# A two-layer graph network on one core: last projection by row block, feature norm from a known variance, f16 counts, first expert pair's weights in dead memory, two gather places

## The chip, the cores and the metric

The kernel runs on one core of one Trainium2 chip. The metric is device time in microseconds. The kernel before took 1129.6 us (median of 3 runs, 1129.23 to 1130.72). All matrices are float32 unless said otherwise.

## The reference, cut to what matters

x has 384 rows of 1024 numbers. There are two layers; each adds two branches to x and then a mixture of experts. In layer 0 every row goes to two of eight experts of width 352. Layer 1 is where the change lies:

```python
xn = _layernorm(x)
x = x + _L1_gnn_ref(xn, ...) + _L1_mix_ref(xn[None], ...)[0]
x = x + _L1_ffn_ref(_layernorm(x)[None], ...)[0]

def _L1_mix_ref(inputs, W_Q, W_K, W_V, W_fc, gamma, beta):
    Q, K = sigmoid(inputs @ W_Q), sigmoid(inputs @ W_K)   # 16 heads of 64
    V = inputs @ W_V
    KV = einsum('bnhk,bnhv->bhkv', K, V)
    num, den = einsum(Q, KV), einsum(Q, K.sum(axis=1)) + 1e-08
    out = (num / den) @ W_fc
    x = out + inputs
    return (x - mean(x)) * rsqrt(var(x) + 1e-05) * gamma + beta

def _L1_ffn_ref(x, centroids, w1, b1, w2, b2, gamma, beta):   # 8 experts, 1024 -> 512 -> 1024
    eid = argmax(x @ centroids.T, axis=1)                     # one expert for each row
    xhat = (x - mean(x)) * rsqrt(var(x) + 1e-05)
    h = xhat * gamma[e] + beta[e]                             # e: the row's expert
    y = x + relu(h @ w1[e] + b1[e]) @ w2[e] + b2[e]
    alpha = sigmoid(x @ centroids[e])
    return alpha * y + (1 - alpha) * x
```

The x of `_L1_ffn_ref` is already normalised, so that its second norm is a norm of a norm.

## The kernel before, in words

Every engine has its own program; they are ordered by semaphores alone. The 384 rows are three blocks (b = 0, 1, 2) of 128. Weights come as a stream of 0.5 MB chunks [128 x 1024] into a ring of 8 slots (`ring`, line 369); a slot is loaded again when `chunk_used` tells that PE has read it. All loads of weights stand in order in SP's queue. A chunk holds two products of 128 x 512 for each block of rows; an f32 product is two PE instructions.

**The mix branch of layer 1.** After Q, K and V, DVE builds eight head pairs: `attend(a)` on PE gives numerator and denominator (L1319), DVE divides (L1899 to L1901) and counts `num_taken`. Then comes the projection W_fc, 8 chunks. PE takes the left half of the columns (slots 0 to 3) for all three blocks together (`chunk_N`, L963, banks 2 to 4), then the right half (slots 4 to 7) by block (`block_rows`, L939, banks 5 to 7). DVE adds the residual to the left halves of all blocks, then for each block: right half (L1915), statistics, the reciprocal deviation by a square root on ACT (`seed`, L641) and one Newton step (L1423 to L1430), scale and add into `xr` (L1920, L1921), statistics of `xr`, again the deviation, and `xn` (L1443). After all three blocks DVE takes statistics of `xn` and writes the features to Y[2].

**The routing of layer 1.** As `xn` comes, PE transposes each block (L920), ACT evicts it (L647), PE multiplies by the centroids (`logits`, L928). DVE finds the first maximum (`first_max`, L1647 to L1653) and writes a one-hot matrix A; PE counts the rows ahead of each row with f32 matrices of zeros and ones (`rank_rows`, L1123, L1126); DVE makes one-hot slots (L1703) and PE the lists of rows (`list_rows`, L1134, f16). A list in `idx` (L1681, L1689) lets POOL gather rows of the features from `xs` in DRAM, where ACT's queue stored them (L636). Layer 0 uses the same functions `first_max`, `rank_rows`, `list_rows` and `route`; there `first_max` runs twice.

**The pairs of layer 1.** Experts go two at a time (four pairs, 64 rows for each expert), both at once in the two halves of PE's columns. For a pair: gather into `Xg` (L559), 8 transposes (`turn_pair_rows`, L1390), 16 small activations on ACT with gamma and beta (`pair_rows_T`, L833), up pass (`up_pair`, L1358, 32 instructions, 8 chunks `w1`), 4 transposes (L1170), relu on ACT (L845), down pass (`down_pair`, L1375, 32 instructions, 8 chunks `w2`), the bias rows `b2row` added by DVE (L1735), a store to `ys` (L804). PE's order is: rows of pairs 0 and 1 turned, up 0, rows of 2 turned, hidden 0 turned, up 1, down 0, rows of 3 turned, hidden 1 turned, up 2, down 1, hidden 2 turned, up 3, down 2, hidden 3 turned, down 3. A gather waits until the one place `Xg` has been transposed. At the end POOL gathers back (L559), DVE adds (L1948), and three stores write `out`.

**Weights of the pairs.** `w1` of even pairs goes to the ring, `w2` of even pairs to G; odd pairs use rest of Y, `mask`, `CT`, `xnT` and `rows`. SP loads `w1` of pair 0 as the ring's next group, as the slots come free from W_fc; `w2` of pair 0 after `num_taken` 8, and then, each as its place is dead, `w1` and `w2` of pair 1. `w1` of pair 2 and later is loaded as an up pass frees its place, `w2` as a down pass does; `b2row` has one place, loaded when the pair before has been added (`y_done`), behind the `w2` loads in the queue.

## Time and profile before

| what | us |
|---|---|
| median of 3 runs | 1129.6 |
| the profiled execution's own time | 1129.68 |
| its span, first to last instruction | 1127.9 |
| PE busy | 1004.0 (89%) |
| DVE, ACT, POOL busy | 346.6, 210.2, 319.0 |
| DMA moved | 175.83 MB, mean 156 GB/s |

"Busy" is an instruction's time on its engine; PE's overlaps its weight loads. The chain of waits follows back from the last instruction to what released each step. PEclk is the clock that PE was granted, as a share of 2.4 GHz: 0.50 is 1.2 GHz. The DMA share is the mean over 16 engines.

### The profile page before, as it was taken

What the parts mean: (1) busy time and instruction counts of PE and PEld (TensorE: products, weight loads), DVE (VectorE), ACT (ScalarE), POOL (GpSimd) and SP (SyncE); (2) the same over time, 40 slices, a digit from 0 to 9 for tenths busy, and PEclk for the clock granted to TensorE, in tenths of its full rate; (3) what the DMA queues carried; (4) which work ended last, traced back from release to release, by engine and by line L of the source; (5) the groups of instructions that cost most, each with busy time, mean ns of one, the idle gap of its engine ahead of it and who ended that gap; (6) DMA issues with size and microseconds to landing.
All of it is one profiled execution on the core that took longest, in us unless ns stands there. A gap on an engine that the chain in (4) does not pass through costs nothing.

```text
span 1127.9 us, 9907 instructions
## 1 busy us (share of the span) xinstructions
PE 1004.0 (89%) x3356; PEld 547.4 (49%) x3356; DVE 346.6 (31%) x947; ACT 210.2 (19%) x445; POOL 319.0 (28%) x247
## 2 busy tenths in 40 slices
PE   3999999999999989999779999289999999963983
PEld 2555555555555445444456655144444555452321
DVE  4233472155000458212230111320220555481002
ACT  2113221111111158300111111101011100022410
POOL 3587887788888500000001000200000000001201
PEclk9999999999999999999769999679999999965996
DMA  9956655544544610130638885643232022297994
GB/s 204 254 95 148 130 112 131 146 97 89 135 98 108 214 56 1 38 112 19 242 115 299 327 334 209 218 156 112 94 108 97 7 86 75 74 329 288 380 325 170
DMA packets 64284, 175.83 MB, mean 156 GB/s; under 512 B 22784, under 2 KB 23392, under 8 KB 64112
## 3 DMA queue, kind: packets, MB, share of 16 engines
q1 hardware_dynamic: 39424, 148.13, 40.7%
q0 software_dynamic: 20960, 15.63, 7.9%
q10 hardware_dynamic: 3856, 11.52, 2.7%
q8 instruction: 23, 0.38, 0.1%
q14 instruction: 21, 0.17, 0.0%
HBM read 161.73 MB, written 13.52 MB: 155 GB/s over the span
## 4 chain that ended last, share of the span: by engine, by line
PE 48%; POOL 21%; DMA 11%; issue 9%; DVE 8%; ACT 1%; SPq 0%; DVEq 0%; POOLq 0%
PE bank L963 17%; PE bank L1160 7%; POOL n_hi L506 6%; POOL n_lo L506 6%; PE bank L939 4%; POOL w_lo L506 4%; POOL w_hi L506 4%; PE bank L952 4%; PE bank L1185 3%; PE bank L1375 3%; PE bank L1358 3%; DMA n_hi<-G 3%; DMA n_lo<-count,ridx 2%; DMA Y<-xs,idx 2%; DMA n_hi<-count,ridx 2%
## 5 line engine op out<-in xcount | busy, mean ns | idle before, releaser
L952 PE MATMUL bank<-xnT,ring 128*128 128x384 f32 x896 | 292.0, 486 | 3.6 <-DMA ring<-in_stream 1.7
L952 PEld LDWEIGHTS bank<-xnT,ring 128*128 128x128 f32 x896 | 170.0, 190 | 122.6 <-issue 2.4
L559 POOL DMA_INDIRECT Y<-xs,idx x12 | 11.4, 953 | 576.7 <-DMA xs<-Y 283.5
L963 PE MATMUL bank<-ring,xnT 128*128 128x512 f32 x288 | 126.3, 601 | 0.7 <-ACT xnT L647 0.7
L963 PE MATMUL bank<-ring,Y 128*128 128x512 f32 x240 | 104.7, 594 | 0.8 <-DVE Y L1901 0.8
L963 PEld LDWEIGHTS bank<-ring,xnT 128*128 128x128 f32 x288 | 55.4, 193 | 70.4 <-issue 69.3
L506 POOL DMA_INDIRECT n_lo<-count,ridx x48 | 83.8, 1746 | 18.7 <-issue 13.7
L506 POOL DMA_INDIRECT n_hi<-count,ridx x48 | 80.2, 1671 | 16.2 <-issue 13.7
L952 PE MATMUL bank<-Y,ring 128*128 x256 | 82.7, 486 | 0.0
L1160 PE MATMUL bank<-ring,Y 128*128 128x352 f32 x256 | 79.2, 468 | 0.7 <-issue 0.7
L963 PEld LDWEIGHTS bank<-ring,Y 128*128 128x128 f32 x240 | 45.2, 190 | 58.5 <-issue 56.3
L679 ACT ACTIVATE Y<-bank,sbias,scale 128x384 f32 (+1 forms) x48 | 32.2, 671 | 206.3 <-PE bank L952 206.3
L952 PEld LDWEIGHTS bank<-Y,ring 128*128 128x128 f32 x256 | 48.6, 190 | 33.9
L939 PE MATMUL bank<-ring,Y 128*128 128x512 f32 x144 | 62.7, 593 | 0.0
L1160 PEld LDWEIGHTS bank<-ring,Y 128*128 128x128 f32 x256 | 49.1, 194 | 27.5 <-issue 2.8
L506 POOL DMA_INDIRECT w_lo<-wts,kidx x48 | 52.6, 1096 | 30.4 <-DMA n_hi<-G 16.1
L506 POOL DMA_INDIRECT w_hi<-wts,kidx x48 | 52.6, 1096 | 14.7 <-issue 14.3
L920 PE MATMUL bank<-k,xn 128*128 128x128 f32 x72 | 14.9, 376 | 33.6 <-DVE xn L1443 33.6
L939 PEld LDWEIGHTS bank<-ring,Y 128*128 128x128 f32 x144 | 27.1, 190 | 33.0 <-issue 33.0
L559 POOL DMA_INDIRECT Y<-ys,idx x9 | 8.5, 947 | 112.5 <-DMA ys<-Y 110.4
L1492 DVE SCALAR_TENSOR_TENSOR CT<-rows,keyf,k 128x128 bf16<-128x128 f32 x80 | 22.7, 351 | 47.3 <-DMA rows<-keys 46.4
L1546 DVE SCALAR_TENSOR_TENSOR G<-G,mask 128x1152 f32<-128x1152 f32 x1 | 2.6, 2604 | 102.7 <-DMA G<-n_hi 102.7
(270 smaller groups left out, 1016.0 us busy)
## 6 DMA issues: line engine op xcount, KB each, us to landing
ring<-in_stream SPq DMA_DIRECT2D x144, 512.0 KB, 3.7
ring<-in_up SPq DMA_DIRECT2D x32, 704.0 KB, 5.8
Y<-in_stream SPq DMA_DIRECT2D x18, 512.0 KB, 14.0
G<-in_stream SPq DMA_DIRECT2D x16, 512.0 KB, 12.3
ring<-in_dn SPq DMA_DIRECT2D x7, 1024.0 KB, 5.8
ys<-Y ACTq DMA_DIRECT2D x12, 512.0 KB, 6.9
rows<-keys SPq DMA_DIRECT2D x10, 512.0 KB, 5.6
xnT<-in_stream SPq DMA_DIRECT2D x6, 512.0 KB, 14.9
```

The source lines that it names most:

```text
L506: pool.indirect_dma_start(table, bass.IndirectOffsetOnAxis(ap=at[:, e:e + 1], axis=0), what[:, e:e + 1], None, **how).then_inc(done, 16)
L559: pool.indirect_dma_start(dst, None, src, bass.IndirectOffsetOnAxis(ap=idx[:, col:col + 1], axis=0))\
L679: act.activation(dst, bank[m % 2][:, 0:N], ACT.Identity, bias=bi, scale=sc).then_inc(t_evicted, 1)
L920: last = pe.transpose(bank[i][:, k * P:(k + 1) * P], xn[:, b, (4 * i + k) * P:(4 * i + k + 1) * P], ident)
L939: last = pe.matmul(bank[5 + b][:], lhs(2 * (r % 4) + k, b), ring[:, r, k * 512:(k + 1) * 512], start=(start and r == slots[0] and k == 0), ...
L952: last = pe.matmul(bank[to][:, 0:N], ring[:, r, k * P:(k + 1) * P], rhs(k), start=(k == 0), stop=(k == KB - 1))
L963: last = pe.matmul(bank[2 + 3 * half + b][:], lhs(k0 + k, b), ring[:, r, k * 512:(k + 1) * 512], start=(start and k == 0), stop=(stop and ...
L1160: last = pe.matmul(bank[2 + h][:, 0:F0], x_, W[:, o:o + F0], **se)
L1185: last = pe.matmul(bank[5 + half][:], h_, w_, start=(f == 0), stop=(f == 2))
L1358: last = pe.matmul(bank[2][a * HC:(a + 1) * HC, :], XgT[i % 2][:, 2 * j + k, a * HC:(a + 1) * HC], w1_of[i][4 * a + j][:, k * 512:(k + 1) ...
L1375: last = pe.matmul(bank[5 + half][a * HC:(a + 1) * HC, :], hT[:, 2 * kk + k, a * HC:(a + 1) * HC], w2_of[i][4 * a + j][:, k * 512:(k + 1) ...
L1492: last = stt(junk[:, t, :], src, keyf[:, bass.ds(e, 1)], same, ALU.is_equal, ALU.mult, accum_out=ndup[:, bass.ds(e, 1)])
```

## The change

- The projection W_fc goes by row block: block 0 left half and right half (its first slots need only some of the heads), block 1, block 0's transposes, block 2's left half, block 0's logits, block 2's right half, and then blocks 1 and 2 are transposed and multiplied.
- DVE does each block to the end: after `xn` it takes the variance of `xn` as var x rstd^2 (no statistics pass), and writes that block's features over z in Y[3]. ACT stores each block as it comes. The multiplication by the gamma row stands before the wait for the seed.
- The counts use f16 copies `later16`, `ones16` (257 more columns in `k16`) and a 24-column f16 copy A16 of A; A3 is written after it. `first_max` has one instruction less (the comparison adds 100 itself); `route` reads ranks from the bank at once and one-hot columns start at 1, so that the subtraction goes; copy of ranks and the maximum come after the first slots.
- `w1` and `w2` of pair 0 go to memory that is dead during W_fc (Y[4], `mask`, `CT`, Y[5], G, `rows`) and are loaded between the ring's last chunks; `w1` of odd pairs goes to the ring, `w2` of odd pairs to Y[3], `xnT` and Y[2]; the latter waits for gathers 0 and 1.
- There are two gather places, `Xg` and G[8192:9216]. The rows of pair 1 are turned in the middle of up pass 0. DVE does the second half of the rows' eviction (`v_rows_T`), ACT the first.
- Nine semaphores become three with offsets.

```diff
+        w1_even = thirds(Y[:, 4, :]) + [flat[0][:, 0:1024], flat[1][:, 0:1024], Y[:, 5, 1024:2048], g8[1], g8[2]]
+        w2_even = g8[3:7] + [rows[:, 1, :], g8[0], g8[7], rows[:, 0, :]]
+        w1_odd = [ring[:, r, :] for r in range(SLOTS)]
+        w2_odd = thirds(Y[:, 3, :]) + thirds(flat[2]) + thirds(Y[:, 2, :])[0::2]
+        Xgs = [Xg, g8[8]]
...
-            sp.wait_ge(num_taken, 8)
             for r in range(SLOTS):
+                next_chunk(CH_F1 // 8 - 1, r)
+                if r == 3:
+                    sp.wait_ge(product_taken, PR_NUM + 1)
+                if r >= 3:
+                    for n in range(2 * r - 6, 2 * r - 4):
+                        if n < SLOTS:
+                            load_first_w1(n)
+                        else:
+                            load_w2(0, n - SLOTS)
+            for r in range(2, 5):
+                load_w2(0, r)
+            sp.wait_ge(product_taken, PR_NUM + 8)
+            for r in range(5, 7):
                 load_w2(0, r)
             load_b2(0)
-            for r in range(5):
+            for r in range(SLOTS):
+                sp.wait_ge(chunk_used, CH_F1 - 7 + r)
                 load_w1(1, r)
             sp.wait_ge(xn_ready, 4 * NB)
-            for r in range(6):
-                load_w2(1, r)
-            sp.wait_ge(pe_output, AFF)
-            for r in range(5, 8):
-                load_w1(1, r)
-            sp.wait_ge(xs_stored, 96)
-            for r in range(6, 8):
+            load_w2(0, 7)
+            sp.wait_ge(M1s.gathered, 16)
+            sp.wait_ge(odd_gathered, 16)
+            for r in range(SLOTS):
                 load_w2(1, r)
...
-                    else:
-                        pool.wait_ge(S.xt_ready, 2 * e)
-                    gather(Xg, xs, e, S.gathered)
+                    elif e >= n:
+                        pool.wait_ge(S.xt_ready, 2 * (e - n + 1))
+                    gather(places[e % n], xs, e, S.gathered if e % n == 0 else odd_gathered)
...
+            three_seeds(0)
+            store_features(0)
             evict_block(TP0 + 4 * NB, 0)
+            three_seeds(1)
+            store_features(1)
             evict_block(TP0 + 4 * NB, 1)
+            three_seeds(2)
             evict_block(TP0 + 4 * NB, 2)
+            store_features(2)
...
+            def fc_first_block(half):
+                for r in range(4 * half, 4 * half + 4):
+                    pe.wait_ge(landed[r], arr(4)(r))
+                    if half == 0:
+                        pe.wait_ge(product_taken, PR_NUM + 2 * r + 2)
...
+            for half in range(2):
+                fc_first_block(half)
+            for half in range(2):
+                fc_block(1, half)
+            turn_block(T_FE, 3 * NB, 0)
+            fc_block(2, 0)
+            pe.wait_ge(zf_done, 2)
+            logits(T_FE, cent, NE, 0)
+            fc_block(2, 1)
+            for b in range(1, NB):
                 turn_block(T_FE, 3 * NB, b)
-                if b == 0:
-                    pe.wait_ge(zf_done, NB)
                 logits(T_FE, cent, NE, b)
...
+                    if i == 0 and j == 2:
+                        turn_pair_rows(1)
...
-                v.tensor_reduce(cmax, bank[2][:, 120:128], AX.X, ALU.max)
-                step(v.tensor_copy(rank, bank[2][:, 96:120]))
-                step(stt(posm, rank, 1.0, small(168, 24), ALU.add, ALU.mult))
-                step(ts(posm, posm, -1.0, None, ALU.add))
+                step(stt(posm, bank[2][:, 96:120], 1.0, small(168, 24), ALU.add, ALU.mult))
...
+            def v_rows_T(i):
+                v.wait_ge(M1s.xt_ready, 2 * i + 2)
+                for k in range(4):
+                    for a in range(2):
+                        g = 8 * (2 * i + a) + 4 + k
+                        last = ts(XgT[i % 2][:, 4 + k, a * HC:(a + 1) * HC],
+                                  bank[pair_banks(i)[1]][:, k * P + a * HC:k * P + (a + 1) * HC],
+                                  cols[:, C_GAM + g:C_GAM + g + 1], cols[:, C_BET + g:C_BET + g + 1], ALU.mult, ALU.add)
+                last.then_inc(upper_done, 1)
...
                 aggregate(b)
-                rstd_of(7 + 2 * b, b, b + 1)
+                ts(ve[:, b:b + 1], mv[:, b:b + 1, 1], EPS, None, ALU.add).then_inc(var_ready, 1)
                 step(stt(z3[:, b, :], z3[:, b, :], mv[:, b, 0:1], rows[:, 0, :], ALU.subtract, ALU.mult))
+                rstd_from(7 + 3 * b, b, b + 1)
...
+                step(stt(ve[:, b:b + 1], rstd[:, b:b + 1], rstd[:, b:b + 1], mv[:, b, 1:2], ALU.mult, ALU.mult))
+                ts(ve[:, b:b + 1], ve[:, b:b + 1], EPS, None, ALU.add).then_inc(var_ready, 1)
+                rstd_from(9 + 3 * b, b, b + 1)
+                v.wait_ge(xn_ready, 3 * NB + b + 1)
+                ts(xh[:, b, :], xn[:, b, :], rstd[:, b:b + 1], None, ALU.mult).then_inc(xh_ready, 1)
-            v.wait_ge(xn_ready, 4 * NB)
-            rstds(13, xn)
-            normalise(YN(2), xn, xh_ready)
```

## Rows read from the trace of the kernel before

**Rows 1.** The page, part 1: busy time, share of the span, instructions.

```profile
...
PE 1004.0 (89%) x3356; PEld 547.4 (49%) x3356; DVE 346.6 (31%) x947; ACT 210.2 (19%) x445; POOL 319.0 (28%) x247
...
```

**Rows 2.** The chain of waits, in order of time: start us, us, what.

```profile
...
571.84 4.28 DMA Y<-xs,idx
...
1012.53 10.74 DMA xs<-Y
...
1024.02 7.47 DMA Y<-xs,idx
...
1034.27 4.36 DMA Y<-xs,idx
...
1101.60 8.91 PE bank L1375 x32
...
```

**Rows 3.** Windows: length, busy us (instructions) by engine, PEclk, DMA share, GB/s.

```profile
...
905.00:946.00 41.00, 41.00 (x129) 24.17 (x128) 22.53 (x19) 4.71 (x8) 0.00 (x0) 1.00 0.24 81
...
1017.00:1031.00 14.00, 1.78 (x18) 1.52 (x17) 4.66 (x20) 0.00 (x0) 0.96 (x1) 0.50 1.03 415
...
1044.00:1051.00 7.00, 7.00 (x40) 2.98 (x38) 0.69 (x1) 0.90 (x5) 0.00 (x0) 1.00 0.87 307
1051.00:1079.00 28.00, 28.00 (x138) 10.04 (x136) 2.67 (x4) 12.71 (x48) 7.95 (x4) 1.00 1.03 413
...
1096.00:1101.00 5.00, 0.00 (x0) 0.00 (x0) 0.79 (x2) 1.52 (x8) 0.00 (x0) 0.75 0.27 74
...
```

**Rows 4.** Timeline of DVE at the end of pair 2.

```profile
...
1100.21 1.29 DVE L1735 TENSOR_TENSOR Y<-bank,Y 128x512 f32<-128x512 f32 x2 [11.65 <-DMA Y<-in_b]
...
```

**Rows 5.** Timeline of PE: start us, us, engine, line, operation, tiles, count.

```profile
...
524.35 1.04 PE L920 MATMUL bank<-k,xn 128*128 128x128 f32 x8
...
532.09 1.86 PE L928 MATMUL bank<-wqkv,xnT 128*128 128x24 f32 x16
...
565.72 2.73 PE L1123 MATMUL bank<-Y,k 128*128 128x8 f32 x12 [6.89 <-DVE Y L1824]
568.30 1.43 PE L1126 MATMUL bank<-Y,k 128*128 128x8 f32 x6
...
949.26 19.15 PE L963 MATMUL bank<-ring,Y 128*128 128x512 f32 x44 [0.82 <-DVE Y L1901]
...
1006.70 3.58 PE L928 MATMUL bank<-cent,xnT 128*128 128x8 f32 x16 [0.69 <-ACT xnT L647]
...
1021.27 0.40 PE L1134 MATMUL bank<-k,Y 128*128 128x1 f16 x9 [1.52 <-DVE Y L1703]
...
1040.57 8.69 PE L1358 MATMUL bank<-ring,Y 128*64 128x512 f32 x32
...
1066.00 7.09 PE L1358 MATMUL bank<-ring,Y 128*64 128x512 f32 x32
...
```

**Rows 6.** Timeline of DVE around the routings and the last projection.

```profile
...
571.40 0.16 DVE L1681 CAST idx<-bank 128x1 uint32<-128x1 f32 x1 [0.34 <-PE bank L1134]
...
952.30 0.56 DVE L1901 TENSOR_TENSOR Y<-bank,Y 128x384 f32<-128x384 f32 x1
...
975.32 0.69 DVE L1915 TENSOR_TENSOR Y<-bank,xn 128x512 f32<-128x512 f32 x1 [3.19 <-PE bank L939]
...
983.88 0.81 DVE L1443 TENSOR_SCALAR xn<-xr,mv,rstd 128x1024 f32<-128x1024 f32 x1
...
1003.18 0.81 DVE L1443 TENSOR_SCALAR xn<-xr,mv,rstd 128x1024 f32<-128x1024 f32 x1
...
1012.41 0.17 DVE L1933 COPY Y<-bank 128x24 f32<-128x24 f32 x1
...
```

**Rows 7.** DMA issues, 515 to 556 us: KB each, median us to landing.

```profile
...
xs<-xn ACTq DMA_DIRECT2D x3, 512.0 KB, 2.7
...
```

**Rows 8.** Timeline of ACT: the eviction of pair 1's transposed rows.

```profile
...
1039.83 4.83 ACT L833 ACTIVATE Y<-bank,cols 128x64 f32<-128x64 f32 x16 [2.31 <-PE bank L1390]
...
```

**Rows 9.** Timeline of SP: the first reload of weights in the pairs.

```profile
...
1044.16 6.05 SPq L451 DMA_DIRECT2D ring<-in_stream  x8
...
```

More of the change, by code:

```diff
@@ L86 @@
 T_FE = T_Q + 8
+D_FC = NB - 1
+N_K = 2 * NB
+N_V = N_K + 2 * NB
+PR_KV = 2 * NB
+PR_NUM = PR_KV + 8
 EW, GL, G2, ZE, EL, AF = range(1, 7)
@@ L931, in logits, with block_rows @@
                     last.then_inc(pe_output, 1)
-            def block_rows(b, slots, lhs, arrived, start, stop):
+            def block_rows(b, slots, lhs, arrived, start, stop, half=1):
                 for r in slots:
@@ L938, in block_rows @@
                     for k in range(2):
-                        last = pe.matmul(bank[5 + b][:], lhs(2 * (r % 4) + k, b), ring[:, r, k * 512:(k + 1) * 512],
+                        last = pe.matmul(bank[2 + 3 * half + b][:], lhs(2 * (r % 4) + k, b), ring[:, r, k * 512:(k + 1) * 512],
                                          start=(start and r == slots[0] and k == 0),
@@ L1293, in _ @@
             for half in range(2):
-                pe.wait_ge(v_done, 3 * half + 3)
+                pe.wait_ge(hkv_done, N_V + 3 * half + 3)
                 for b in range(NB):
@@ L1328, in _, with attended, fc_block @@
             attend(7)
-            def fc_first(k, b):
-                if k == 0 and b == 2:
-                    pe.wait_ge(num_taken, 7)
-            for kk in range(4):
-                if kk == 3:
-                    pe.wait_ge(num_taken, 8)
-                chunk_N(kk, tok(2), 2 * kk, 0, arr(4)(kk), kk == 0, kk == 3, fc_first if kk == 0 else None)
-            for b in range(NB):
-                block_rows(b, range(4, 8), tok(2), arr(4)(4), True, True)
-            for b in range(NB):
+            def attended(k):
+                return tok(2)(k, 0)
+            def fc_first_block(half):
[3 more added lines that the diff above has]
+                        pe.wait_ge(product_taken, PR_NUM + 2 * r + 2)
+                    for k in range(2):
+                        last = pe.matmul(bank[2 + 3 * half][:], attended(2 * (r % 4) + k), ring[:, r, k * 512:(k + 1) * 512],
+                                         start=(r % 4 == 0 and k == 0), stop=(r % 4 == 3 and k == 1))
+                last.then_inc(block_done, 1)
+            def fc_block(b, half):
+                block_rows(b, range(4 * half, 4 * half + 4), tok(2), 0, True, True, half)
+            for half in range(2):
[8 more added lines that the diff above has]
+            for b in range(1, NB):
                 turn_block(T_FE, 3 * NB, b)
-                if b == 0:
-                    pe.wait_ge(zf_done, NB)
                 logits(T_FE, cent, NE, b)
@@ L1665, in one_hot_slots @@
                 for b in range(NB):
-                    last = ts(slot[:, b, e, :], iota[:, 0:CAP], where[:, b * 8 + e:b * 8 + e + 1], None, ALU.is_equal)
+                    last = ts(slot[:, b, e, :], iota[:, 1:CAP + 1], where[:, b * 8 + e:b * 8 + e + 1], None, ALU.is_equal)
                 return last
@@ L1746, in b2_arrived @@
                     v.wait_ge(b2_in, 32 * i + 32)
+                for i in range(2):
+                    v_rows_T(i)
                 v_hidden(M1s, 0, 1, step)
+                v_rows_T(2)
                 for i in range(1, PAIRS):
@@ L1822, in _ @@
             first_max(lg3, m2, oh2)
-            tt(A3, oh1, oh2, ALU.add).then_inc(R0.assigned, 1)
+            tt(A16, oh1, oh2, ALU.add).then_inc(R0.assigned, 1)
+            step(tt(A3, oh1, oh2, ALU.add))
             tt(dlt, m2, m1, ALU.subtract).then_inc(act_input, 1)
```

195 lines of the change are left out of this document (98 added, 97 removed).

## The prediction

> **What bounds the kernel now.** I read part 1 of the page, then the chain of waits over the last 180 us, then the stretches by window, and last the instructions of PE and DVE one by one there. The page shows PE busy for 89% of the span [rows 1], so most of the kernel is matmul time which the change leaves alone. The chain shows where it is not: from the last projection to the end it leaves PE for DVE, for the store of the features (10.74 us), for two gathers (7.47 and 4.36 us), and then for the last down pass at 1101.60 [rows 2]. The windows say why the store and the first gather are long: the DMA engines are full (415 GB/s, share 1.03) from 1017 to 1031, PE's granted clock is 0.50 there, while from 905 to 946 the same engines had stood at 0.24 [rows 3]. From 1051 on they are full again at 413 GB/s, and the end of that backlog, the bias rows of pair 2, is what DVE waits for at 1100.21, and down pass 3 for DVE [rows 3, 4]. So the tail has two limits in turn: latency up to the first pair, DMA bytes after it.
>
> **The change part by part.** All times are in the old trace's us until the sum.
>
> Layer 0's routing. Nine f32 rank products (18 instructions) run from 565.72 to 569.73, 4.01 us, nothing beside them [rows 5]. In f16 they are 9 instructions. The nearest row is the f16 list product, nine instructions of one column in 0.40 us; the far bound is that an f16 instruction costs what an f32 one does, 9 x 0.22 = 2.0 us. I take 0.5 by the nearer row: gain 3.5. Each first_max loses one instruction at 0.21 (two calls: 0.42); in `route` the copy of the ranks and the subtraction leave the path (0.3 + 0.2 = 0.5), the copy and the maximum now lie under PE's list product. Added: one A3 sum, under the rank products. Sum 4.4 (2.9 to 4.6). The expert loop behind it keeps PE busy without waits for DMA, so I let this stay gained; its cover is PE's alone.
>
> Constants. 257 more f16 columns are 66 KB, 0.16 us at the full rate of [rows 3], at a lower one early on perhaps 0.5; behind them wait the table fills that release POOL. I take 0.3 lost (0 to 0.6). Merging semaphores costs nothing: the same increments in the same order.
>
> The projection. 96 instructions at 0.435 us [rows 5] remain 41.8 us. It starts at 946.6: slots 0 to 2 of block 0 take 5.2 us to 951.8, slot 3 waits for DVE's last head at 952.86 [rows 6], stall 1.1 where the old order had 0.8. Block 0 is whole at 961.5 (it was at 975.3), block 1 at 975.3; then block 0's transposes (0.87 at the full clock), half of block 2, block 0's logits (1.7) [rows 5] and the other half: 991.8 instead of 989.0. PE's path is 2.8 longer, but only DVE needs it. DVE takes 9.37 from the second half's addition to xn (975.32 to 984.69) [rows 6]; now the product with the gamma row covers the seed, about 0.4 less: 8.95. Block 0 has xn at 970.5, its features 2.5 later (two small ops 0.4, seed and Newton steps 1.3, the 0.8 multiplication); block 1's features are ready at 986.8; block 2's first half is taken by 988.2 and DVE then waits for PE until 991.8. Its xn comes at 1000.8 (old 1003.99) and its features at 1003.3 (old 1012.50, after three statistics passes and a common multiplication, just as DVE turned to the logits at 1012.41 [rows 6]). ACT is in order too: block 1's eviction must be over before the seed of block 2; by PE's times it is, by 0.2 us, at 993.7. If it is late, DVE waits that much.
>
> The store. Blocks 0 and 1 are stored earlier; the last starts at 1003.6. The DMA engines then hold nearly nothing (next step), so I take the 2.7 us of layer 0's stores [rows 7] and some issue time, 3 in all, instead of 10.74 [rows 2]: 1006.6. This is no longer last: the list of rows is.
>
> Routing of layer 1. Transpose, eviction and logits of block 2 took from 1003.99 to 1010.3 [rows 5, 6]; now from 1000.8 to 1007.1. DVE is free and copies at once; assignment to rank took 1.67, less 0.2: 1008.6. Rank 0.5: 1009.15 (bound 1010.65). From the end of the rank products to the written index layer 0 shows 1.83 [rows 5, 6]; less 0.5: 1010.45. The gather lands 4.55 after the index in layer 0 (571.56 to 576.12) [rows 2, 6]: 1015.0 against 1031.5. The second list is known 1.9 after the first and the second gather has a place of its own, so it doesn't wait for transposes: landed 1016.9 against 1038.63.
> Beside this the Trainium skill (SBUF — State Buffer, section SBUF: two separate sides) says that a DVE operation in a two-port mode locks GpSimd out, and with it the writing of a gather's descriptors. Layer 0's row disagrees here: that gather landed in 4.28 us with f16 one-hot operations all through it [rows 2]. By the rule the first gather could lose the 1.35 us of the second one-hot operation; by the row nothing. I add nothing.
>
> First pair. Transposes 1.97 at the low clock: 1017.0. The eviction is split: ACT's 8 at 0.30 [rows 8], DVE's 8 of 128x64 out of PSUM are not in the trace; between 0.15 (smallest operations) and 0.45 (128x512 takes 0.69) each, I take 0.2: 1.6. Up pass 0 starts at 1018.6 (old 1040.57). It took 8.69, the first part at clock 0.5, full by 1044 [rows 3, 5]; with pair 1's transposes inside (1.0) and a slightly longer slow part, its end is 1028.6 against 1049.27: PE is 20.7 ahead. Gather 2, which PE needs there, now starts at 1017.3 into full queues: by the first gather's 7.47 us [rows 2] at 1024.8, and even behind the whole 4.2 MB at 1028.9, 0.3 late. From there each pass is 7.0 as before [rows 5].
>
> Weights. Pair 0 (16 chunks of 0.5 MB, save one) is loaded from about 917 to 960, at three chunks per 6.45 us, 244 GB/s in place of 81, under the 413 that the engines reach [rows 3]; ring chunks come first in each round, and need a slot freed by PE, as before: no cost. Pair 1's first weights go into the ring between 978 and 996. Pair 1's second weights wait for both gathers: from 1016.9. Here is the price. Before, all of pair 1 was in place when pass 0 began; now 4.2 MB are still to come and gather 2 is 0.5 MB more: 4.7 MB / 0.413 = 11.4 us of extra backlog. The old backlog ran from the first reload at 1044.16 [rows 9] to the bias rows at 1100.21 [rows 4], 56.0 us, of which 1044 to 1051 moved 307 instead of 413 GB/s, a loss of 1.8 that won't recur as the queue is never empty. New end: 1016.9 + 56.0 - 1.8 + 11.4 = 1082.5. PE's feeding on the way: pair 1's second weights land by 1028.6 (needed 1052), pair 2's first by 1040 (1045.9), pair 3's first by 1050 (1060), pair 2's second by 1061.5 (1067): all in time. PE alone would reach down pass 3 at 1076.4 (its last hidden rows were evicted at 1097.5, the old waits for pair 2 were 0.5); the bias rows let DVE finish pair 2 at 1083.8, so **the last down pass starts 17.7 us earlier** than 1101.60, again after a pause and at the low clock, so it again takes 8.91 [rows 2]. All after it is unchanged, 26.3 us to the span's end.
>
> Sum: 17.7 + 4.4 - 0.3 = 21.8. Span 1127.9 - 21.8 = 1106.1; the profiled run's own time is 1129.68, 1.78 above its span and 0.08 above the median of 1129.6: **1107.9 us**.
>
> **Rivals.**
> A. PE sets the end. The bias rows are 0.5 MB at the tail of a queue; if they pass the weights, or the queue empties sooner, down pass 3 starts at 1076.4 plus nothing: 25.2 instead of 17.7, time 1100.4. For: PE is that far ahead. Against: DVE sat idle 11.65 us for such rows [rows 4], with a smaller backlog beside the same PE work.
> B. Latency ahead of the gathers. Everything behind gather 1 shifts one for one. If the order on ACT and DVE (a seed behind an eviction behind PE's transposes) delays block 2, if f16 rank costs 2.0 in both layers, or if the store still meets loads, 4 to 7 us return: 1112 to 1115, middle 1113.
> C. Nothing comes of it: pair 1's loads, started late, give back all. The backlog would have to last 22 us longer, 9 MB at 413 GB/s; I find 4.7. Time 1129 or so.
> D. Slower: PE's clock. PE idles more thinly spread before pass 0 now; if the granted clock stays at 0.5 (1.2 GHz) through the pairs, each of the seven passes before the last down pass takes 14 instead of 7: it starts at about 1076.4 + 45 = 1121, and itself takes 14 instead of 8.9: end 1127.9 + 20 + 5 - 4 = 1149, time about 1150. It decides from the third slow pass on. Against: at the same point, with the same kind of work, the clock was back by 1044 and stayed at 1.00 to 1079 [rows 3].
> The Trainium skill (TensorE: Matmul & The Clock Gate, section Seeing it yourself) notes a clock seen stuck at a low level for a long time; no row here shows that.
>
> **How the numbers follow.** Forecast 0.62, A 0.16, B 0.14, C 0.03, D 0.05. The likeliest case's own bounds: rank and routing 1.7, eviction 1, backlog 2: 1104 to 1112. With A and B the range is 1099.5 to 1114. A difference over 0.2% is about what can be told from none here (2.3 us): faster 0.92, same 0.03, slower 0.05.
>
> **What the profile after would show.** Rank products of about 0.5 us in both layers; the feature store 3 us; both gathers before the first up pass, 2 us apart; DMA at 0.5 or more from 917 to 946 (old clock) and nearly none from 1000 to 1012; up pass 0 starting 26 us earlier by its own trace; DMA full from then to about 1078, and DVE waiting for bias rows once more before down pass 3. Wrong would be: a PE wait inside the projection, a wait of PE on weights of pairs 1 to 3, DVE waiting for ACT's seed of block 2, or no wait before down pass 3 (A).

## The result and the profile after

The changed kernel takes 1112.14 us (median of 4 runs, 1111.22 to 1114.94) against 1130.16 for the kernel before on the same chip (4 runs, 1129.23 to 1133.93): ratio 0.9834, interval 0.9813 to 0.9855. The forecast was 1107.9, with a range of 1099.5 to 1114. The profiled execution took 1111.84, its span is 1110.0 (before: 1129.68 and 1127.9), so the span lost 17.9 us where the forecast's sum says 21.8.

The measured time is at the upper edge of the forecast's own bounds (1104 to 1112) and also in the band of rival B (1112 to 1115), so the time alone doesn't decide between them; the traces have to.

Two numbers organise all that follows. **Upstream**: DVE's last head ends at 952.86 before [rows 6] and 949.73 now: 3.1 us gained. **Tail**: from there to the end of the span, 175.0 us before, 160.3 now: 14.8 gained. In the experiments the tail is counted from PE's next product, 0.12 us later; there the changed kernel has 160.15. Times of the new trace plus 3.1 are in the clock of the prediction.

The page, part 1, after (as [rows 1]): PE's work is only 5.5 us less, of a gain of 17.9. Most of the gain is waiting.

```profile
PE 998.5 (90%) x3338; PEld 539.8 (49%) x3338; DVE 351.5 (32%) x979; ACT 201.4 (18%) x415; POOL 319.7 (29%) x247
```

The chain of waits after, in order of time (start us, us, what), over the same stretch as [rows 2]:

```profile
949.85 8.82 PE bank L1365 x20
958.67 13.73 PE bank L966 x32
...
1007.75 5.58 DMA Y<-xs,idx
1013.37 1.13 PE bank L1396 x4
1014.53 2.48 ACT Y L855 x8
...
1017.59 5.13 PE bank L1416 x16
...
1058.61 7.02 PE bank L1416 x32
1065.62 4.43 issue
1070.05 9.63 PE bank L1433 x32
...
1080.31 1.75 ACT Y L867 x8
1082.06 2.10 issue
1084.16 8.80 PE bank L1433 x32
```

The store of the features, 10.74 us in [rows 2], is gone from the chain; of the gathers only the first is left in it, 5.58 us instead of 7.47. Up pass 0 starts at 1017.59 (1020.7 in the old clock, 1040.57 before [rows 5]). Then PE runs without a gap to 1065.62, and then the chain shows "issue" of 4.43 and 2.10 us ahead of down passes 2 and 3. A bank that DVE has not emptied yet shows as issue here; DVE's timeline (start us, us, engine, line, operation, tiles, count, idle before and releaser) says why it had not:

```profile
1068.66 1.29 DVE L1782 TENSOR_TENSOR Y<-bank,Y 128x512 f32<-128x512 f32 x2 [16.77 <-DMA Y<-in_b]
...
1082.77 1.29 DVE L1782 TENSOR_TENSOR Y<-bank,Y 128x512 f32<-128x512 f32 x2 [12.22 <-DMA Y<-in_b]
```

The kernel before had both waits too, pair 2's in [rows 4] and pair 1's here, but pair 1's rows came late by so little that down pass 2 lost only 0.51 us (1087.56 to 1088.07):

```profile
1086.67 1.29 DVE L1735 TENSOR_TENSOR Y<-bank,Y 128x512 f32<-128x512 f32 x2 [12.85 <-DMA Y<-in_b]
```

Now PE is ready for down pass 2 22 us sooner and the bias rows of pair 1 come only 18 us sooner, and the same wait costs down pass 2 4.43 us. The windows (length, busy us and instructions of PE, PEld, DVE, ACT, POOL, then PEclk, DMA share, GB/s) show the transfers' side, to be held against [rows 3]:

```profile
917.00:946.00 29.00, 29.00 (x90) 16.70 (x89) 17.81 (x16) 3.24 (x5) 0.00 (x0) 1.00 0.71 257
1003.00:1009.00 6.00, 1.97 (x25) 1.71 (x25) 3.68 (x14) 0.22 (x1) 1.25 (x1) 0.50 0.00 0
1015.00:1029.00 14.00, 11.75 (x56) 5.00 (x56) 5.51 (x20) 4.64 (x16) 4.44 (x4) 0.80 0.94 362
1029.00:1061.00 32.00, 32.00 (x156) 11.45 (x154) 6.19 (x18) 9.79 (x40) 4.44 (x2) 1.00 1.03 410
1061.00:1067.00 6.00, 4.62 (x22) 1.29 (x18) 0.00 (x0) 0.00 (x0) 0.00 (x0) 1.00 1.05 226
1077.00:1083.00 6.00, 3.27 (x18) 1.11 (x14) 0.23 (x1) 1.74 (x8) 0.00 (x0) 1.00 0.44 102
1068.00:1074.00 6.00, 3.95 (x10) 1.37 (x12) 1.89 (x3) 0.00 (x0) 0.00 (x0) 0.53 1.03 410
```

Read the last two columns together. From 917 the loads of pair 0 run under the projection at 257 GB/s, and PE is busy for all 29 us. From 1003 to 1009 nothing moves: the first gather finds the engines empty. From 1017 on they are full. But from 1061 to 1067 the share is 1.05 and the rate only 226 GB/s: full engines that carry half. This is where the two loads of the bias rows of pair 1, 64 partitions each, stand in the queue; they are 0.5 MB of the 1.4 MB that move in these 6 us. The kernel before has the same dip ahead of the same rows:

```profile
1079.00:1086.00 7.00, 7.00 (x36) 2.41 (x34) 0.00 (x0) 1.74 (x8) 0.00 (x0) 1.00 1.03 260
```

Last, PE and POOL around the two routings (same columns as DVE's timeline):

```profile
565.66 0.32 PE L1149 MATMUL bank<-Y,k 128*128 128x8 f16 x6 [6.48 <-DVE Y L1887]
565.84 0.22 PE L1152 MATMUL bank<-Y,k 128*128 128x8 f16 x3
...
571.83 1.97 PE L1171 MATMUL bank<-k,Y 128*128 128x128 f32 x8 [0.69 <-DMA Y<-xs,idx]
574.53 10.78 PE L1186 MATMUL bank<-ring,Y 128*128 128x352 f32 x26 [0.73 <-issue]
```

```profile
1007.40 1.35 DVE L1750 TENSOR_TENSOR Y<-k,Y 128x1152 f16<-128x1152 f16 x1
```

```profile
1007.75 1.83 POOL L580 DMA_INDIRECT Y<-xs,idx  x1 [270.75 <-DVE idx L1728]
1009.89 0.94 POOL L580 DMA_INDIRECT G<-xs,idx  x1 [0.31 <-issue]
```

The rank products take 0.4 us instead of 4.01 [rows 5]. And POOL's first gather instruction takes 1.83 us, the second 0.94; the first one started inside DVE's long one-hot operation.

### The profile page after: what moved, and what is told of

Read it like the earlier page. It is cut to its first block, busy times and chain, and to the rows that moved or that the text cites. A ratio compares the mean times of both kernels' runs of the same rounds, so it can differ in the third digit from the quotient of the medians.

```text
span 1110.0 us, 9830 instructions
## 1 busy us (share of the span) xinstructions
PE 998.5 (90%) x3338; PEld 539.8 (49%) x3338; DVE 351.5 (32%) x979; ACT 201.4 (18%) x415; POOL 319.7 (29%) x247
## 4 chain that ended last, share of the span: by engine, by line
PE 51%; POOL 23%; issue 9%; DVE 8%; DMA 7%; ACT 2%; ACTq 0%; DVEq 0%; POOLq 0%
PE bank L990 15%; PE bank L1186 7%; POOL n_hi L527 7%; POOL n_lo L527 7%; PE bank L966 6%; POOL w_lo L527 4%; POOL w_hi L527 4%; PE bank L979 4%; PE bank L1211 3%; PE bank L1433 3%; PE bank L1416 3%; DMA n_hi<-count,ridx 3%; PE bank L1078 2%; PE bank L1323 1%; DMA Y<-xs,idx 1%
## 5 line engine op out<-in xcount | busy, mean ns | idle before, releaser
L527 POOL DMA_INDIRECT n_lo<-count,ridx x48 | 82.7, 1722 | 17.7 <-issue 13.7
L990 PE MATMUL bank<-ring,Y 128*128 128x512 f32 x192 | 83.6, 594 | 0.0
L966 PE MATMUL bank<-ring,Y 128*128 128x512 f32 x160 | 70.0, 593 | 0.0
L1186 PEld LDWEIGHTS bank<-ring,Y 128*128 128x128 f32 x256 | 49.5, 196 | 27.8 <-issue 3.4
L990 PEld LDWEIGHTS bank<-ring,Y 128*128 128x128 f32 x192 | 36.2, 190 | 46.0 <-issue 45.8
L966 PEld LDWEIGHTS bank<-ring,Y 128*128 128x128 f32 x160 | 30.0, 190 | 35.9 <-issue 35.9
```

The source lines that it names most:

```text
L527: pool.indirect_dma_start(table, bass.IndirectOffsetOnAxis(ap=at[:, e:e + 1], axis=0), what[:, e:e + 1], None, **how).then_inc(done, 16)
L966: last = pe.matmul(bank[2 + 3 * half + b][:], lhs(2 * (r % 4) + k, b), ring[:, r, k * 512:(k + 1) * 512], start=(start and r == slots[0] a ...
L990: last = pe.matmul(bank[2 + 3 * half + b][:], lhs(k0 + k, b), ring[:, r, k * 512:(k + 1) * 512], start=(start and k == 0), stop=(stop and ...
L1186: last = pe.matmul(bank[2 + h][:, 0:F0], x_, W[:, o:o + F0], **se)
```

## The experiments

The theories. **Theory 1**: the end is set by the bytes queued behind gather 1, and by the bias rows at their tail; the shortfall against the forecast lies in the slow bias loads, either because their source is one row broadcast to 64 partitions (1a) or because a load of 64 partitions carries half (1b). **The rival**: it is latency ahead of the gathers (evictions, the collision on POOL) that came back late, and everything behind shifts with it. All ratios are against the kernel before, run on the same chip; the kernel as changed has 0.9834. As upstream varies by some us from profile to profile, the tails of the profiles (160.15 as changed) are a second comparison. A tail is one execution, and it holds the last down pass, which took from 7.11 to 9.94 us in the variants of the changed kernel as the granted clock in it differed; so the table behind the experiments also gives the start of down pass 3.

**All of the first pair's eviction on ACT.** DVE's half (`v_rows_T`) goes back to ACT.

```diff
-            def v_rows_T(i):
-                v.wait_ge(M1s.xt_ready, 2 * i + 2)
...
+                for h in range(2):
+                    act.wait_ge(M1s.xt_ready, 2 * i + h + 1)
+                    for k in range(4):
+                        for a in range(2):
+                            last = act.activation(...)
```

> The changed kernel with one part undone: ACT evicts all 16 pieces of a pair's transposed rows, DVE none. Theory 1 (the end is set by the bytes queued behind gather 1; PE runs ahead and waits): up pass 0 starts about 2.4 us later than 1017.6 (8 more activations at 0.3), but the last down pass starts within 0.5 us of 1084.2 and the time stays within 0.7 us of 1112. Rival (PE's chain from the first pair on sets the end): the time grows by the same 2.4 us, and the last down pass starts at 1086.6.

Measured: 1111.78 us (4 runs, 1108.79 to 1113.73), ratio 0.9832 (0.9802 to 0.9862), tail 161.1. The chain of that kernel:

```profile
1017.74 2.46 issue
1020.20 5.72 PE bank L1417 x16
...
1068.83 2.65 issue
1071.47 8.78 PE bank L1434 x32
...
1082.64 2.72 issue
1085.36 8.80 PE bank L1434 x32
```

Up pass 0 waits longer and starts 1.8 us later than with the split by that profile's own upstream (2.6 less 0.8), and down pass 2 then waits 2.65 instead of 4.43. The delay was eaten by slack before the bytes' end: the rival falls for delays behind the gathers, theory 1 stands.

**Bias rows repeated in DRAM.** Same two loads of 64 partitions, but each of their rows read from its own copy.

```diff
-                    sp.dma_start(b2row[a * HC:(a + 1) * HC, :], b2_d[2 * i + a].to_broadcast([HC, D]))
+                    sp.dma_start(b2row[a * HC:(a + 1) * HC, :], b2_d[2 * i + a, 0:HC, :])
```

> The changed kernel, but each expert's bias row lies 128 times in DRAM (laid out beforehand), so that the load reads 64 different rows instead of one row 64 times; same bytes, same place in the queue. In the changed kernel the DMA rate falls from 412 to about 225 GB/s for 6 us from 1061 to 1067, when the bias rows of pair 1 move. Theory 1a (reading one DRAM row 64 times is slow, 2.7 us for each pair beyond its bytes): the dip goes, the bias rows of pair 1 land about 3 us earlier (1065.5), down pass 2 starts within 1.5 us of up pass 3's end (it had waited 4.4), the rows of pair 2 about 5 us earlier; total 4 to 6 us less. Rival (the low rate comes from the destination, 64 partitions, or from a store beside it): nothing changes, within 0.7 us.

Measured: 1110.19 us (4 runs, 1109.44 to 1113.25), ratio 0.9836 (0.9807 to 0.9864), tail 160.9: nothing. Its window 1059 to 1065 (columns as above):

```profile
1059.00:1065.00 6.00, 4.80 (x24) 1.35 (x20) 0.00 (x0) 0.00 (x0) 0.00 (x0) 1.00 1.03 222
```

Theory 1a falls: the dip is there without a broadcast.

**Bias rows of a pair in one load.** Laid out beforehand as 128 rows for each pair, one load of 128 partitions; the bytes are the same.

```diff
-                for a in range(2):
-                    sp.dma_start(b2row[a * HC:(a + 1) * HC, :], b2_d[2 * i + a].to_broadcast([HC, D]))
+                sp.dma_start(b2row, b2p_d[i]).then_inc(b2_in, 16)
```

> The changed kernel, but the bias rows of a pair come in one load of 128 partitions from a DRAM tensor laid out beforehand, in place of two loads of 64 partitions; same bytes, same place in the queue. With repeated rows but two loads of 64 partitions the dip of the DMA rate had stayed (186 to 260 GB/s for 6 us). Theory 1b (a load into 64 partitions moves at half rate or less; the Trainium skill, SBUF — State Buffer, section Door 1: The DMA port swizzle, says that a range of 64 partitions reaches half of the ports): no dip, rows of pair 1 land 2 to 3 us earlier, rows of pair 2 about 5; last down pass at 1079 to 1080 instead of 1084.2, total 4 to 5 us less than the changed kernel's 1112. Rival (the rate falls because of what else is in flight, stores and descriptors): within 0.7 us.

Measured: 1107.6 us (4 runs, 1105.87 to 1109.25), ratio 0.9777 (0.9733 to 0.9821), tail 156.7. A window, then the chain:

```profile
1059.00:1065.00 6.00, 6.00 (x30) 1.87 (x26) 0.00 (x0) 0.97 (x5) 0.00 (x0) 1.00 1.03 410
```

```profile
1065.21 1.31 issue
1066.52 7.09 PE bank L1431 x32
...
1075.98 3.18 issue
1079.17 9.94 PE bank L1431 x32
```

At the same share of 1.03 the engines carry 410 instead of 222 GB/s, the wait for pair 1's rows shrinks to 1.31 us, and down pass 2 takes 7.09 instead of 9.63, all of it at the full clock. Down pass 3 starts 4.65 us sooner, counted as the tail is; its own clock fell, it took 9.94 instead of 8.80, and so the tail shows 3.45 of that. Theory 1b stands, with two reservations: the edit changes the width of a load and the number of loads together, and by time alone the intervals of the ratios just overlap (0.9821 and 0.9813). That these loads are slow doesn't yet make them the reason why the forecast missed; the point on the backlog below says why they are not. This is also what the Trainium skill says (SBUF — State Buffer, section Door 1: The DMA port swizzle): a transfer to 64 partitions reaches only half of the ports. The trace agrees (226 against 410 GB/s), and adds that such loads in a full queue about halve the rate of the whole core, not only their own.

**Pair 1's second weights loaded as their places die**, partly ahead of the gathers, instead of all after gather 1.

```diff
-            sp.wait_ge(M1s.gathered, 16)
-            sp.wait_ge(odd_gathered, 16)
-            for r in range(SLOTS):
-                load_w2(1, r)
...
+            sp.wait_ge(xs_stored, 96)
+            for r in range(3):
+                load_w2(1, r)
+            sp.wait_ge(pe_output, AFF)
+            for r in range(3, 6):
+                load_w2(1, r)
```

> The changed kernel, but the second weights of pair 1 are loaded as their places die (one chunk after the projection, four at the last features' store, three after the affinities) and no longer wait for the two gathers. Theory 1 (bytes): 4 MB leave the backlog; gathers slow down by 1 to 3 us each as they meet these loads, up pass 0 starts 1 to 3 us later, but down passes 2 and 3 no longer wait for bias rows (4.4 and 2.1 us, and 2.8 at the low clock); total 4 to 7 us less. Rival (latency up to the first pair counts one for one): total 1 to 3 us more.

Measured: 1108.16 us (4 runs, 1106.95 to 1109.33), ratio 0.9806 (0.978 to 0.9833), tail 158.0. The first gather now meets loads (PE waits 6.60 us for it, issued at 1007.03, landed about 1015.0), up pass 0 starts at 1019.30, and still the end comes 2.2 us sooner by the tail: down pass 2 doesn't wait at all. Again latency lost and bytes gained, and the bytes win. The gain is less than the 4 to 7 us expected, 3.2 by the ratios (whose intervals overlap): down pass 3 still waited for the bias rows of pair 2, 4.18 us behind its hidden rows.

**Both of these together.**

> The changed kernel with both: pair 1's second weights loaded as their places die, and the bias rows in one load of 128 partitions. Early second weights alone gave 1108.2 (down pass 2 no longer waited, down pass 3 waited 6.0 us for bias rows at a falling rate). Theory 1 with 1b: down pass 3 follows its hidden rows with 0 to 2 us of wait and keeps more of the full clock; 4 to 7 us less than 1108.2, that is 1101 to 1104. Rival (the bias load is late for another reason, its issue after pair 1's output): 1107 to 1108.

Measured: 1105.51 us (4 runs, 1102.13 to 1108.98), ratio 0.9758 (0.9708 to 0.9809), tail 153.8. Now the last wait before down pass 3 has another releaser:

```profile
1069.25 6.87 PE bank L1440 x32
...
1076.74 1.33 ACT Y L874 x6
...
1078.54 8.81 PE bank L1440 x32
```

It is ACT's relu of pair 3's hidden rows, which is in PE's own chain: the bytes no longer set the end. The gains of the two edits by the tail, 2.15 and 3.45, add up to 5.6 of the 6.4 seen together; by the start of down pass 3, 2.2 and 4.65 are 6.9 of 6.4 (their ratios, 0.9806 and 0.9777 against 0.9758, have overlapping intervals). The expectation, 1101 to 1104, was narrowly missed.

**The collision on POOL.** The 18 one-hot columns after the first slots as single tensor_scalar instructions, in place of one f16 tensor_tensor of 128x1152.

```diff
-                    half_slots(2, NE).then_inc(R.slots, 1)
+                    for e in range(2, NE):
+                        for b in range(NB):
+                            last = ts(hslot[:, b, e, :], iota[:, 1:HC + 1], posm[:, b * 8 + e:b * 8 + e + 1], None,
+                                      ALU.is_equal)
+                    last.then_inc(R.slots, 1)
```

> The changed kernel, but the later slots of layer 1's routing are written by 18 tensor_scalar instructions on DVE instead of one tensor_tensor with two operands in SBUF. In the changed kernel POOL's first gather instruction takes 1.83 us instead of 0.94 and starts while that tensor_tensor (1.35 us) runs; in layer 0 the same instruction runs beside tensor_scalar and takes 0.94. Theory (the tensor_tensor holds GpSimd back): POOL's instruction takes 0.94 to 0.97, the first gather lands about 0.9 us sooner after its list than now (5.6 us from the instruction's start becomes 4.3 to 4.7), the second list is 1 to 2 us later. Rival (the first use of a far address, or an instruction load, makes it long): 1.83 stays.

Measured, one run: 1113.01 us, tail 161.05. POOL's timeline:

```profile
1007.94 0.96 POOL L580 DMA_INDIRECT Y<-xs,idx  x1 [270.59 <-DVE idx L1728]
1011.28 0.94 POOL L580 DMA_INDIRECT G<-xs,idx  x1 [2.38 <-DVE idx L1740]
```

The instruction is back at 0.96 us, and PE has its rows at 1012.34 instead of 1013.37. So the 0.9 us were a collision with that tensor_tensor. But 18 instructions are slower than one, gather 1 goes out 1.4 us later and with it all bytes behind it, and the end is no better: down pass 2 waits 5.83. The collision is real and not what sets the time here.

**The last form of this.** With both edits of bytes and the scalar slots:

> The early second weights and the bias rows in one load (1105.5), plus only the later slots by tensor_scalar. Theory: POOL's first gather instruction is 0.96 instead of 1.84 us, that gather lands about 0.9 earlier or, where the queues are what it waits for, not at all earlier; the list for pairs 1 to 3 is 1.5 us later, which nobody waits for as pair 1's rows are turned only in the middle of up pass 0. Total 0 to 1 us less than 1105.5.

Measured: 1108.28 us (5 runs, 1106.01 to 1109.29), ratio 0.9789 (0.9767 to 0.981), tail 151.9. No gain over the version without the scalar slots (0.9758, interval overlapping), where 0 to 1 us was expected: down pass 3 starts at the same point of the tail (127.8 and 127.95), and the shorter tail is the last pass, 7.11 us here at the full clock and 8.81 there. And with pair 1's three chunks for `xnT` held back until gather 0 has landed:

```diff
             sp.wait_ge(pe_output, AFF)
+            sp.wait_ge(M1s.gathered, 16)
             for r in range(3, 6):
```

> The early second weights and the bias rows in one load of 128 partitions (1105.5), plus later slots by tensor_scalar, and three of the early chunks held until the first gather has landed. In the kernel of 1105.5 the first gather took 8.2 us from its instruction, in the queues' way, and no weights or bias rows were waited for at the end (down pass 3 waited 1.8 us for its own hidden rows). Theory: the gather is back at 4.5 to 5.5 us, up pass 0 starts 2.5 to 4 us earlier; but the bytes held back end later, so that bias rows of pair 2 are waited for again, 1 to 3 us: total 0 to 3 us less than 1105.5. Rival (PE's chain was the only limit by now): 3 to 4 us less.

Measured: 1105.47 us (5 runs, 1103.06 to 1106.91), ratio 0.9756 (0.9733 to 0.9778), tail 150.1, which is 24.8 less than in the kernel before and 10 less than in the changed one. It beats both kernels: the intervals are apart (as changed 0.9834, 0.9813 to 0.9855). The ratios don't tell it from the version without the added wait (0.9789), whose interval overlaps, nor from the version with the two edits of bytes alone (0.9758); in its one profile down pass 3 starts some 3.7 us sooner than in either. PE waits 1.60 us for gather 0 instead of 4.74, and of bias rows only pair 1's are still waited for by DVE, ahead of PE's need:

```profile
1064.02 1.29 DVE L1794 TENSOR_TENSOR Y<-bank,Y 128x512 f32<-128x512 f32 x2 [7.88 <-DMA Y<-in_b2p]
...
1076.79 1.29 DVE L1794 TENSOR_TENSOR Y<-bank,Y 128x512 f32<-128x512 f32 x2 [6.17 <-PE bank L1441]
```

**One part at a time.** Four runs ask what each part of the change is worth.

The 15 early loads of pair 0 moved behind the projection:

```diff
-                if r >= 3:
-                    for n in range(2 * r - 6, 2 * r - 4):
-                        ...
...
+            sp.wait_ge(chunk_used, CH_F1)
+            for r in range(SLOTS):
+                load_first_w1(r)
+            for r in range(7):
+                load_w2(0, r)
```

> The changed kernel, but all 15 early loads of pair 0's weights wait until the projection has been computed; places in memory and everything else are the same. Theory 1 (the gain of the change in layer 1 is mostly that these 7.9 MB move while the DMA engines are idle, under the projection): the store of the features takes 8 to 11 us again, the first gather 7 or more, up pass 0 starts 6 to 9 us later, the end 6 to 10 us later than the changed kernel's: 1118 to 1122. Rival (the gain comes from the row order, the short feature norm and the gathers; the DMA engines have room enough after the projection): within 2 us of 1112.

Measured: 1123.25 us (7 runs, 1120.23 to 1129.35), ratio 0.991 (0.9882 to 0.9937), tail 173.1. The chain of the old kernel is back:

```profile
1004.63 8.09 DMA xs<-Y
...
1013.48 9.29 DMA Y<-xs,idx
...
1075.93 10.80 issue
1086.73 9.95 PE bank L1425 x32
```

This profile was the slowest of the seven runs. By its tail 13.0 of the 14.8 us hang on these loads, by the ratios of all runs 8.6 of 18.8 (0.991 against 0.9834, whose intervals are apart), in three places: the store, the gather, and the backlog.

One gather place instead of two:

```diff
-        Xgs = [Xg, g8[8]]
+        Xgs = [Xg]
```

> The changed kernel with one part undone: a single gather place, so that the second gather waits for pair 0's transposes, and the second weights of pair 1 wait for it. Theory 1 (bytes behind the second gather set the end): the second gather lands at about 1020 instead of 1015, PE's up pass 0 is not held up by it, the end is 5 us later: about 1117. Rival (PE's chain): 0 to 1 us later.

Measured: 1117.86 us (4 runs, 1116.9 to 1119.18), ratio 0.9872 (0.9846 to 0.9898), tail 164.6: 4.5 us worse. Gather 1 is issued at 1017.55 instead of 1009.89 and PE waits 4.74 us for gather 2. (The parts overlap: by the tails 13.0 and 4.5 are more than 14.8.)

The features' variance by a pass of statistics again:

```diff
-                step(stt(ve[:, b:b + 1], rstd[:, b:b + 1], rstd[:, b:b + 1], mv[:, b, 1:2], ALU.mult, ALU.mult))
+                half_stats(xn, b, 0)
+                step(half_stats(xn, b, 1))
+                aggregate(b)
```

> The changed kernel with one part undone: the features' variance of each block comes from two statistics instructions and an aggregation over xn again. DVE needs 1.2 us more for each block. Theory: blocks 0 and 1 hide it, block 2's features come at 1001.3 and their store lands by 1004.5, before the list of rows (1007.5), so that the features cost nothing; but ACT's seed for them now stands 1.2 us later ahead of its eviction of block 2's transposes, which moves the list by 0.5 to 1.0 us: 0 to 1.5 us in all, against a measurement that can't tell it from nothing by time, only by the trace. Rival (the short norm carries a good part of the gain, 3 to 4 us): 1115 or more.

Measured: 1115.45 us (4 runs, 1114.37 to 1116.28), ratio 0.9847 (0.9822 to 0.9873), tail 160.2. No difference that can be told, and the tail is the same: with the store out of the chain the features may come later, since the list of rows is what gathers wait for.

The f16 counts alone, in the kernel before:

```diff
+        A16 = w[:, 800:812].bitcast(F16).rearrange("p (b e) -> p b e", b=NB)
-                                  later if a == b else ones, A[:, a, :],
+                                  later16 if a == b else ones16, A16[:, a, :],
```

> The kernel before with one part of the change alone: f16 rank products, the shorter first maximum and the shorter head of the routing, in both layers. Theory: layer 0 gains 4.5 us (its rank products 3.5, DVE 0.9), of which the expert loop may give back 1; in layer 1 nothing, because there the features' store, landing at 1023.3, is later than the list of rows at 1020: total 3.5 to 4.7 less. Rival (layer 1's counts are on the path too): 8 us less.

Measured: 1125.46 us (9 runs, 1123.04 to 1126.84) against 1129.77, ratio 0.9962 (0.9949 to 0.9975): 4.3 us (2.8 to 5.8). In layer 1 of that kernel the store and not the index is last before the gather [rows 2], so this is layer 0's routing, which the forecast put at 4.4.

**The profiles side by side**, in us. The start of down pass 3 and the tail are both counted from PE's first product after DVE's last head; each row is one execution, the ratio is over all runs.

| version | ratio | down pass 3 starts | it takes | tail |
|---|---|---|---|---|
| as changed | 0.9834 | 134.3 | 8.80 | 160.15 |
| eviction on ACT | 0.9832 | 134.7 | 8.80 | 161.1 |
| bias rows repeated | 0.9836 | 134.9 | 8.80 | 160.9 |
| bias rows in one load | 0.9777 | 129.7 | 9.94 | 156.7 |
| second weights early | 0.9806 | 132.1 | 8.80 | 158.0 |
| both | 0.9758 | 127.95 | 8.81 | 153.8 |
| both, scalar slots | 0.9789 | 127.8 | 7.11 | 151.9 |
| both, scalar slots, added wait | 0.9756 | 124.15 | 8.81 | 150.1 |
| scalar slots alone | one run | 135.1 | 8.80 | 161.05 |
| loads late | 0.991 | 146.4 | 9.78 | 173.1 |
| one gather place | 0.9872 | 138.9 | 8.69 | 164.6 |
| norm by statistics | 0.9847 | 134.4 | 8.80 | 160.2 |

## Why the prediction was right, and what it mis-sized

The direction, the limits and their order were right. Step by step, in the prediction's own clock (new trace plus 3.1):

- **Layer 0's routing**, forecast 4.4. PE's transposes of the first expert start 4.3 us sooner (571.83 against 576.16 in the trace before); PE reached that layer's affinities 0.35 late, so the step itself gave 4.7. The f16 price taken from the list products was right: 0.4.
- **"I let this stay gained"** failed by 1.0 us. From those transposes to the loop's end took 129.0 us, before 128.0. After the shorter routing the granted clock stayed at 0.50 for 5.75 us of the first up pass (574.53 to 580.28), before for 4.2 (578.86 to 583.04). The cause is read off the trace, not tested.
- **Constants**, forecast 0.3 lost. The fills release POOL at 36.10, before at 36.27: nothing.
- **Projection, `xn`, index.** Stall 1.12 (forecast 1.1), block 0 whole at 961.8 (961.5), `xn` of block 2 at 1001.0 (1000.8), index at 1010.6 (1010.45). All within 0.3. ACT's seed delayed nothing.
- **The store** is out of the chain, and 1003 to 1009 has 0 GB/s, as said. In the experiment with the late loads the store takes 8.09 us and is back in the chain, so this is due to the early ones.
- **Gather 0**, "I add nothing": landed at 1016.5, forecast 1015.0. 0.9 of it is the collision with DVE, shown by the scalar slots. The prediction took layer 0's row for evidence, but the one-hot operations beside which that gather took its short time are tensor_scalar, and in layer 1 it is a tensor_tensor, which is not one of the two-port operations of the rule that the prediction quoted either. The Trainium skill (SBUF — State Buffer, section Who interferes with whom) says that a tensor_tensor with both inputs in SBUF contends with GpSimd's reads, and infers that it leaves the writing of descriptors alone. The trace bears out a contention, 1.83 us beside it and 0.96 beside tensor_scalar; whether the gather's reads or its descriptors waited, no run separates, and the instruction was late as a whole.
- **Eviction**: DVE's eight pieces took 2.11 us (0.26 each), forecast 1.6, so up pass 0 starts at 1020.7 instead of 1018.6. The cost of these 2.1 us was smaller than their size, as the next point decides.
- **The backlog** is the mis-sized term. "New end: 1082.5" for the bias rows of pair 2: DVE has them at 1085.9, and down pass 3 starts at 1087.3 instead of 1083.8, which is 14.3 sooner than before and not 17.7. Gather 1 landed 1.3 us later than forecast (about 1018.2 against 1016.9), and that part shifted about one for one (with one gather place, where gather 1 was issued 5.8 us later by that profile's own upstream, down pass 3 started 4.6 later). The other 2.1 us are in the backlog's length, 67.7 us instead of the 65.6 of the sum 56.0 - 1.8 + 11.4. The windows of the whole backlog, before, then after with its first 1.9 us:

```profile
1044.16:1100.21 56.05, 51.07 (x248) 18.69 (x244) 5.25 (x8) 16.93 (x66) 7.95 (x4) 0.98 0.96 352
1015.09:1082.77 67.68, 58.50 (x266) 21.20 (x264) 13.59 (x41) 16.08 (x63) 8.88 (x5) 0.91 0.96 357
1015.09:1017.00 1.91, 0.25 (x2) 0.00 (x0) 1.62 (x7) 1.91 (x7) 0.90 (x1) 0.50 0.50 103
```

That is 19.7 MB and 24.2 MB. The added bytes, 4.4 MB, were put right (4.7, 11.4 us at 413 GB/s; 4.4 are 10.7). What failed is "a loss of 1.8 that won't recur as the queue is never empty": the queue was empty when gather 1 landed, since pair 1's second weights wait for it, and the first 1.9 us ran at 103 GB/s, which costs 1.4; all in all the rate lost 0.9 us more than before, where the sum has 1.8 less. The slow form of the bias loads is not the reason for the miss. It cost the new backlog 6 x (413 - 226) / 413 = 2.7 us ahead of pair 1's rows, but the old one 7 x (413 - 260) / 413 = 2.6, so the 56.0 us of the sum already held it. What the experiment with one load shows is what mending it brings, 4.65 us at down pass 3, and not where the forecast's 3.4 went.
- **"All in time"** failed: the list of what feeds PE named the weights and left out the bias rows of pair 1. The trace before had shown the wait: the 0.5 that the prediction calls "the old waits for pair 2" is down pass 2 waiting for these rows. They now let it wait 4.43 us, at a place where the forecast has none; then the clock was at 0.53 on average from 1068 to 1074 and the pass took 9.63 instead of 7. By itself this cost nothing more, since PE had slack until the rows of pair 2 came: down pass 3 still waited 2.10. Nor did it hold up the rows of pair 2, whose one place `b2row` came free at 1069.95: the weights ahead of them kept the engines full to about 1077.
- **Behind down pass 3** "unchanged, 26.3": 25.8, 0.5 gained.

The sum: forecast 21.8, less 1.0 (the expert loop), less 3.4 (the end of the backlog), plus 0.5, is 17.9. Of the rivals, B's mechanism (latency) was there: 1.3 us at gather 1, which counted in full, and 2.1 at up pass 0, which mattered little; A's (PE sets the end) became true only once the bias loads and the order of pair 1's weights were mended; C and D did not show: the clock stood at 1.00 from 1029 to 1061. Little of the closeness (0.4% in time) is luck: the two misses, the loop and the end of the backlog, go the same way; 0.5 behind down pass 3 and the 0.7 us of bytes too many within the backlog go the other.

Open: why upstream differs by some us between profiles of like kernels (PE reached one and the same product of layer 0 between 462.1 and 469.8 us). In the two slowest, the loads late and the added wait, PE waited 4.28 and 4.17 us for a chunk of the ring at about 35 us (0.37 in the changed kernel) and the granted clock then stood at 0.50 for 6.8 us; why that chunk was late stays open. Also open: the row-block order by itself wasn't tried; whether the best version is held by anything but PE's chain was not tested; and why the last pass kept the full clock in one profile (7.11 us) and not in others with the same wait of 1.8 us ahead of it (8.81).

## What to carry to other kernels

Where a queue of loads ends on the path, count its bytes, whether the queue is empty when they start, and the form of each load: here two loads into 64 partitions took the whole core from 410 to 226 GB/s. A stretch that is scaled from an old trace brings its old slow loads with it. A list of what must be in time holds every operand of a stage, the small ones above all, since they stand last in the queue. And an early load is worth most where it empties the queue ahead of a latency chain: 15 loads moved under a matmul stretch carried 8.6 us of the gain by the runs' ratios, 13.0 by the tail of one profile.

## What the hardware showed that was not expected

- Two loads of 64 partitions x 4 KB in a full queue: 226 GB/s at a DMA share of 1.05, against 410 at 1.03 for one load of 128 partitions. A high share with a low rate is the sign to look for.
- A POOL indirect gather that starts inside an f16 tensor_tensor of DVE takes 1.83 us instead of 0.94; it ends 0.83 after that operation does, as if it had begun there. Beside tensor_scalar 0.96 (1.01 at most in the runs here).
- A wait of 4.43 us in PE's pairs brought the granted clock to 0.50 again and made a 7 us pass last 9.63; a wait of 1.31 left it at 7.09. Ahead of the last pass a wait of 1.8 us was followed by the full clock and 7.11 us in one profile, and by 3.4 us at 0.50 and 8.81 us in two others.
- In the up pass behind the first routing the low clock lasted longer (5.75 us, before 4.2) where the routing ahead of it was shorter.
